# Feed-forward weights laid out in stationary order, a three-part normalisation on ScalarE, and a second product that runs two tiles behind

## What is computed

```
xn = layernorm(x)                                        # over 512, eps 1e-5
s  = attention(xn, wq, wk, wv, wo)                       # 32 query heads, 8 kv heads, head 128, RoPE, window 128
W1, W3 (1376 x 512), W2 (512 x 1376) = dequant_q40(w, s) # high and low nibble of a packed int, one scale per 64
g  = silu((silu(xn @ W1.T) * (xn @ W3.T)) @ W2.T)
out = x + s * g
```

## Time and profile before

| | us |
|---|---|
| median of 3 runs | 878.67 |
| lowest, highest | 878.37, 880.2 |
| the profiled execution, whole | 877.86 |
| its span in the trace | 876.1 |
| TensorE busy in the span | 840.6 (96%) |
| VectorE, ScalarE, GpSimd busy | 600.6, 469.7, 390.2 |
| granted TensorE clock, mean | 0.998 |

### The profile page before, as it was taken

One profiled execution on the slowest core, in us unless ns is written; L12 is line 12 of the kernel. 1 busy time (PEld: TensorE's weight loads), 2 busy tenths in 40 slices (PEclk: granted clock), 3 DMA queues, 4 the chain that ended last, 5 costly groups with the idle time before them and its releaser, 6 DMA issues.

```text
span 876.1 us, 13995 instructions
## 1 busy us (share of the span) xinstructions
PE 840.6 (96%) x4252; PEld 701.8 (80%) x4252; DVE 600.6 (69%) x1621; ACT 469.7 (54%) x1133; POOL 390.2 (45%) x303
## 2 busy tenths in 40 slices
PE   3999999999989999999999999999999999999887
PEld 3777888888767888888888888888888888888765
DVE  7953554433569677775968586677858676875895
ACT  2474121132577557574756666485748557574641
POOL 0144121124545436552644464184435436552892
PEclk9999999999999999999999999999999999999999
DMA  6200001002010201200120111012000201200211
GB/s 195 56 18 8 13 24 51 19 1 72 1 41 9 74 1 48 73 1 1 48 72 0 48 36 35 0 48 72 0 27 21 72 0 48 72 0 0 61 62 60
DMA packets 40224, 32.55 MB, mean 37 GB/s; under 512 B 5056, under 2 KB 32384, under 8 KB 40192
## 3 DMA queue, kind: packets, MB, share of 16 engines
q1 hardware_dynamic: 40192, 32.16, 12.5%
HBM read 30.05 MB, written 2.10 MB: 37 GB/s over the span
## 4 chain that ended last, share of the span: by engine, by line
PE 82%; DVE 8%; POOL 3%; issue 3%; ACT 3%; DMA 0%; SPq 0%; ACTq 0%; POOLq 0%; DVEq 0%
PE bank L966 25%; PE bank L968 24%; PE bank L967 24%; PE bank L1106 5%; PE bank L1086 3%; DVE probs L815 2%; POOL acc L338 1%; ACT W2raw L433 1%; POOL swap L321 1%; PE bank L986 1%; PE bank L1076 1%; DVE xl L655 1%; POOL acc L342 0%; POOL q L325 0%; DMA xn<-in_L_attn_x 0%
## 5 line engine op out<-in xcount | busy, mean ns | idle before, releaser
L321 POOL TENSOR_TENSOR swap<-swap,cst 128x512 f32<-128x512 f32 x80 | 103.9, 1298 | 248.8 <-ACT swap L488 247.9
L966 PE MATMUL bank<-xh,wih 128*128 128x512 f32 x384 | 158.5, 413 | 0.2 <-DVE q L783 0.2
L968 PE MATMUL bank<-xh,wil 128*128 128x512 f32 x384 | 151.0, 393 | 0.0
L967 PE MATMUL bank<-xl,wih 128*128 128x512 f32 x384 | 150.3, 391 | 0.0
L815 DVE TENSOR_SCALAR probs<-probs,rinv 128x128 f32<-128x128 f32 (+1 forms) x256 | 129.1, 546 | 4.6
L515 ACT ACTIVATE probs<-probs,nmx 128x128 f32<-128x128 f32 (+1 forms) x256 | 113.5, 445 | 33.8 <-DVE nmx L804 33.4
L523 ACT ACTIVATE ph<-bank 128x512 fp32r<-128x512 f32 x96 | 55.6, 597 | 112.2 <-PE bank L1106 110.9
L966 PE MATMUL bank<-woh,oh 128*128 128x512 f32 x256 | 100.4, 392 | 0.3 <-DVE ol L832 0.3
L968 PE MATMUL bank<-woh,ol 128*128 128x512 f32 x256 | 99.9, 390 | 0.0
L967 PE MATMUL bank<-wol,oh 128*128 128x512 f32 x256 | 99.9, 390 | 0.0
L287 POOL TENSOR_TENSOR hl<-act_h,hh 128x512 fp32r<-128x512 f32 x22 | 29.9, 1361 | 148.2 <-ACT hh L416 148.2
(11 more groups left out here) (102 smaller groups left out, 1828.0 us busy)
## 6 DMA issues: line engine op xcount, KB each, us to landing
raw<-in_L_attn_wq SPq DMA_DIRECT2D x32, 256.0 KB, 2.8
raw<-in_L_attn_wo SPq DMA_DIRECT2D x32, 256.0 KB, 2.9
packed<-in_L_ffn_w SPq DMA_DIRECT2D x20, 128.0 KB, 2.2
xn<-in_L_attn_x SPq DMA_DIRECT2D x8, 256.0 KB, 3.5
raw<-in_L_attn_wk SPq DMA_DIRECT2D x8, 256.0 KB, 3.0
raw<-in_L_attn_wv SPq DMA_DIRECT2D x8, 256.0 KB, 2.7
raw<-in_L_attn_x SPq DMA_DIRECT2D x8, 256.0 KB, 2.7
out<-gate SPq DMA_DIRECT2D x8, 256.0 KB, 2.0
```

What stands on the lines that cost most here:

```text
L321: nc.gpsimd.tensor_tensor(v, v, spread(sin.unsqueeze(1), P, 2, SEQ), ALU.mult).then_inc(sin_done, 1)
L966: nc.tensor.matmul(out_, sh, mh, start=(i == 0), stop=False)
L967: nc.tensor.matmul(out_, sh, ml, start=False, stop=False)
L968: m = nc.tensor.matmul(out_, sl, mh, start=False, stop=(i == n - 1))
```

## The change

The host hands the packed weights over in another order: W1 and W3 with the inner dimension on partitions (the packed row of 64 is loaded twice, once for the high and once for the low nibbles), W2 with the hidden dimension on partitions. No value is computed on the host; scales are repeated so that each weight has its own, and the scales of W1 and W3 are spread over 64 partitions by the load itself. Unpacking is a shift left by 24 or 28 (by partition or by column) and an arithmetic shift right by 28, then one multiplication. The result is what the matmuls need, so all transposes of weights go, and the high and low parts are made from SBUF instead of PSUM.

- Normalisation in three parts: tiles 0-1, 2-3 and 4-7; the normalising pass moves to ScalarE (scale and bias). The square-root table is loaded ahead by a dummy activation.
- TensorE begins with tile 0 in quarters of 256 tokens; tiles 0 and 1 run their first halves before their second halves.
- The hidden buffer has four slots; `w2_mult(u)` runs behind tile 2u+3, for every u, and uses four PSUM banks (banks 0 and 1, which the turned weights had, come free).
- W2 is unpacked tile by tile, tile t-2 during tile t; the last three during tile 10, and the loads of them wait for buffers (`load2`).
- The loops over feed-forward tiles are written out.

```
-            def w13_turn(t, s2_):          # 8 transposes for a tile: gone
-            def w2_turn(t):                # 4 transposes for a tile: gone
+            def load13(t, m):
+                wait(sp, W13_done, 2 * t + m - 3)
+                s = t % 2
+                for half in range(2):
+                    rows = slice(half * HALF, half * HALF + HALF)
+                    sp.dma_start(pk[rows, s, m, :], w13[:, t, m, :]).then_inc(w13_in[s][m], 16)
+                    sp.dma_start(sc[rows, s, m, :], s13[half, t, m:m + 1, :].to_broadcast([HALF, PK])) \
+                        .then_inc(w13_in[s][m], 16)
+            def load2(t):
+                wait(sp, W2_done, t - 1)
+                sp.dma_start(pk2[:, t % 2, :], w2[t]).then_inc(w2_in[t % 2], 16)
+                sp.dma_start(sc2[:, t % 2, :], s2[t]).then_inc(w2_in[t % 2], 16)
...
+            def norm(i):                   # ScalarE
+                act.wait_ge(ln_small, 6 * part_of(i) + 6)
+                nc.scalar.activation(xn[:, i, :], xn[:, i, :], ACT.Identity, bias=std[:, 0, i:i + 1],
+                                     scale=std[:, 3, i:i + 1]).then_inc(xn_done, 1)
...
+            for t in range(2, FT - 1):     # ScalarE
                 silu(t, 0)
+                hid_hi(t, 0)
+                w2_hi(t - 2)
                 silu(t, 1)
+                hid_hi(t, 1)
+                if t + 2 < FT:
+                    w13_hi(t + 2, 0)
+                    w13_hi(t + 2, 1)
             silu(10, 0)
+            hid_hi(10, 0)
+            w2_hi(FT - 3)
+            w2_hi(FT - 2)
+            w2_hi(FT - 1)
             silu(10, 1)
+            hid_hi(10, 1)
...
+            def dequant13(t, m):           # VectorE
+                nc.vector.tensor_scalar(nib[:, m, :], pk[:, s, m, :], shc[:, 4:5], shc[:, 5:6],
+                                        ALU.logical_shift_left, ALU.arith_shift_right).then_inc(nib_done, 1)
+                nc.vector.tensor_tensor(W13[:, m, :], nib[:, m, :], sc[:, s, m, :], ALU.mult).then_inc(W13_done, 1)
+            def w13_lo(t, m):
+                nc.vector.tensor_tensor(W13l[:, t % 2, m].rearrange("p t n -> p (t n)"), W13[:, m, :],
+                                        W13h[:, t % 2, m].rearrange("p t n -> p (t n)").bitcast(f32),
+                                        ALU.subtract).then_inc(W13l_done, 1)
+            def dequant2(t):
+                nc.vector.tensor_tensor(nib2[:, :].rearrange("p (e j) -> p e j", j=4),
+                                        pk2[:, s, :].rearrange("p (e j) -> p e j", j=4),
+                                        spread(shc[:, 0:4].unsqueeze(1), P, P, 4), ALU.logical_shift_left)
+                nc.vector.tensor_scalar(nib2[:, :], nib2[:, :], 28, None, ALU.arith_shift_right)
+                nc.vector.tensor_tensor(W2[:, s, :], nib2[:, :], sc2[:, s, :], ALU.mult).then_inc(W2_done, 1)
...
+            for t in range(2, FT):         # VectorE
+                if t + 2 < FT:
+                    dequant13(t + 2, 0)
+                    dequant13(t + 2, 1)
+                hid(t, 0)
+                dequant2(t - 2)
+                if t == FT - 1:
+                    dequant2(t - 1)
+                    dequant2(t)
+                hid(t, 1)
+                if t + 2 < FT:
+                    w13_lo(t + 2, 0)
+                    w13_lo(t + 2, 1)
+                if t > 2 and t % 2:
+                    ffn_add((t - 3) // 2)
...
+            for t in range(2, FT - 1):     # GpSimd
+                hid_lo(t, 0)
+                w2_lo(t - 2)
+                hid_lo(t, 1)
+            hid_lo(FT - 1, 0)
+            w2_lo(FT - 3)
+            w2_lo(FT - 2)
+            w2_lo(FT - 1)
+            hid_lo(FT - 1, 1)
...
+            def w2_mult(u, pair):          # TensorE
+                pe.wait_ge(W2l_done, 2 * u + len(pair))
...
+            x_turn(0)
+            x_turn(1)
+            w13_start(0, 0)
+            x_turn(2)
+            x_turn(3)
+            w13_start(0, 1)
+            w13_start(1, 0)
+            w13_start(1, 1)
+            w13_mult(1, 0, 0, {3: lambda: x_turn(4)})
+            x_turn(5)
+            w13_mult(1, 0, 1, {2: lambda: x_turn(6), 3: lambda: x_turn(7)})
+            for t in range(2):
+                w13_mult(t, 1, 0)
+                w13_mult(t, 1, 1)
+            w13_tile(2)
+            for u in range(FT // 2 - 1):
+                w13_tile(2 * u + 3)
+                w2_mult(u, (0, 1))
+                w13_tile(2 * u + 4)
+            w2_mult(FT // 2 - 1, (0, 1))
```

More of the change, by code:

```diff
@@ L221, in _ @@
[L221 to L230, removed]
+            load13(1, 1)
+            for t in range(2, FT):
+                for m in range(2):
+                    load13(t, m)
+                if t == 2:
+                    sp.dma_start(cst[:, 0:C_ID], const[:, 0:C_ID]).then_inc(const_in, 16)
+                load2(t - 2)
@@ L274, in _, with w13_first @@
         def _(pool):
[L276 to L288, removed]
+            def w13_first(t, m):
+                pool.wait_ge(W13h_done, 2 * t + m + 1)
+                nc.gpsimd.tensor_tensor(W13l[:, t, m].rearrange("p t n -> p (t n)"), W13[:, m, :],
+                                        W13h[:, t, m].rearrange("p t n -> p (t n)").bitcast(f32),
+                                        ALU.subtract).then_inc(W13l_first, 1)
@@ L290, in _ @@
+            for t in range(2):
+                for m in range(2):
+                    w13_first(t, m)
             hid_lo(0, 0)
+            hid_lo(1, 0)
+            hid_lo(0, 1)
             hid_lo(1, 1)
[L292 to L296, removed]
@@ L400, in w13_hi @@
[L400 to L405, removed]
-            def silu(t, half):
-                act.wait_ge(ab_ps, 4 * t + (2 * half + 1))
-                wait(act, hl_done, 2 * t + (half - 1))
-                nc.scalar.activation(act_h[:, half, :], bank[2 + 2 * half][:, :], ACT.Silu).then_inc(silu_done, 1)
@@ new lines, in _ @@
+            x_hi(0)
+            x_hi(1)
+            root(1)
+            norm(2)
+            norm(3)
+            w13_hi(0, 1)
+            x_hi(2)
+            x_hi(3)
+            w13_hi(1, 0)
+            root(2)
+            for i in range(4, NT):
+                norm(i)
+            w13_hi(1, 1)
+            for i in range(4, NT):
+                x_hi(i)
+            silu(0, 0)
+            hid_hi(0, 0)
+            silu(1, 0)
+            hid_hi(1, 0)
+            silu(0, 1)
+            hid_hi(0, 1)
@@ L994, in w13_mult, with w13_start, w13_tile @@
+            def w13_start(m, part):
+                cols = slice(2 * part * P, (2 * part + 2) * P)
+                pe.wait_ge(W13l_first, m + 1)
+                pe.wait_ge(xl_done, 2 * part + 2)
+                i = three(bank[2 + m][:, cols],
+                          [(W13h[:, 0, m, d, :], W13l[:, 0, m, d, :], xh[:, d, cols], xl[:, d, cols])
+                           for d in range(DT)])
+                if part:
+                    i.then_inc(ab_ps, 1)
+            def w13_tile(t):
                 for half in range(2):
-                    wait(pe, h_done, 2 * t + (half - 1))
@@ L1007, in w2_turn @@
[L1007 to L1016 removed]
+                        w13_mult(t, half, m)
```

494 lines of the change are left out of this document (213 added, 281 removed).

## The result

The changed kernel is slower: 886.25 us (median of 6 runs, 881.98 to 886.76) against 878.52 (6 runs, 877.99 to 880.2), ratio 1.007, 95% interval 1.0053 to 1.0087. The forecast was 869.9 with a range to 876. The profiled execution took 883.83 us, its span 881.8; the granted TensorE clock was 0.986 of full speed where it had been 0.998, and in the other five runs 0.983 to 0.990.

A forecast was written before the change was run, and what follows sets the result against it. TensorE, busy 96% of the span, was taken as the bound. Overhead removed 16.0, stalls 9.9, start 1.6 and end 1.1 gave 16.0 - 9.9 + 1.6 + 1.1 = 8.8 us less: 869.1 profiled, 869.9 median, range 861 to 876.

The forecast's parts named there:

- What the removed work is worth: Tile 2 to the attention: 153.4 us of matmuls stay out of 169.4; the other 16.0 are overhead the change removes.
- the stalls: TensorE's new waits for W2's low part, ahead of the five w2_mult: 9.9 us in sum.
- The upper bound of 16: Most the five W2 waits could total: each half as long again and loads 1 us late at every pair.
- The waits: TensorE waiting for W2's low part: 2.3 us for u = 0, 1.3 each for u = 1 to 3, 3.7 in tile 10.
- Rival B: Transfers decide: each pair 1.5 us later still, or the start loses its gain; 2.8 us less, 875.9; chance 0.13.
- Being held: VectorE operations with two SBUF inputs and GpSimd's exclude each other for a whole instruction; dequant2's product held until 9.7.
- The start: Up to tile 2: a chain through VectorE and ScalarE; tile 2 begins at 43.7 instead of 45.30, 1.6 us earlier.
- The two stalls behind it: TensorE's waits before tile 2: 1.6 us for W3's low part and 2.6 for act_h.
- The end: Last single tile of the second product: four banks end TensorE's waits for VectorE's adds, 1.1 us gained.
- C: Slower than before: VectorE becomes the bound of the feed-forward, 20 us lost against 18.7 gained; 880, chance 0.06.

The follow-up runs named there:

- the variant: Changed kernel with W2's unpacking put first in its tile on VectorE, ScalarE and GpSimd: 862.12 us, ratio 0.9816 to the kernel before; 861.12 when run again.
- the filled waits: Changed kernel with 48 extra 512-column matmuls ahead of TensorE's waits for W2's low part: 878.23 us, ratio 0.9994 to the kernel before.
- the loads edit: Changed kernel with W1/W3 loads ahead of the waiting W2 load in SyncE's list: 875.1 us, ratio 0.9957; on top of W2's unpacking first, 861.11 us.
- the half tile: Changed kernel with w2_mult(u), u = 0 to 3, half a tile later in TensorE's list: 872.19 us, ratio 0.9917 to the kernel before.
- put in: Three idle times on TensorE, made by GpSimd fills, added to the kernel with W2's unpacking first: 881.61 us, ratio 1.0025 to the kernel before.
- the start edit: Kernel with W2's unpacking first, plus silu table and W3's high part of tile 1 earlier: 859.15 us, again 860.45; with W1/W3 loads earlier too, 860.02.

## Why the prediction was wrong

Against the profiled execution: forecast 869.1, measured 883.8, 14.7 too little. The median is 16.4 above its forecast: it lies 2.4 above the profiled execution, where I had put it 0.8 above. For these 1.6 us there is no trace.

- **What the removed work is worth: right.** Forecast 153.4 us of matmuls between tile 2 and the attention; without a wait, in the variant, the stretch takes 152.8 (45.54 to 198.39). 16.0 were to be had there.
- **The failed step: the stalls were priced as idle time only.** "Stalls: 3.9 + 2.3 + 3.7 = 9.9." should have been idle time and what it does to the clock. That is 8.1 us, more than half of the error, and the filled waits show them by themselves. Behind the start the kernel before has no slow matmul, and its longest wait there is 1.1 us. But the start had the sign, and I read past it: 16 turns behind the wait of 9.6 us take 3.65, and 16 behind the wait of 2.2 take 2.02. Start to start that is 0.21 us and 0.11, half speed and full. I asked for waits of 1.3 to 3.7 us and left the clock out of the forecast and of the bounds. The upper bound of 16 is also summed too low by its own conditions: half as long again is 14.9, and 1 us more at each of five pairs makes 19.9. The page "TensorE: Matmul & The Clock Gate" of the Trainium skill, section "HAM oscillation — how this bites in real kernels", has the mechanism (a stall sends the engine back to the slow clock, and the next stretch of matmuls starts slow), and I had not weighed it. The runs here agree with it.
- **The waits: right in place and mechanism, too small by 4.** Forecast 2.3, 1.3, 1.3, 1.3, 3.7; measured 4.9, 2.7, 2.7, 0.2, 3.3 (13.9 of idle time, 14.7 in distances between starts). Two terms are off. Rival B's loads were on the path for u = 0 to 2, and with them sent earlier these waits are 2.2, 1.1 and 1.5, close to the forecast: I had given the second W1/W3 load 1 us of margin, with 0.45 us for an issue that takes 0.6, eight in a row. And u = 3 has no `dequant13` ahead of it, as t + 2 is past the last tile; I gave it the same 1.3 as its neighbours. Tile 10 was right.
- **Being held: right.** The product takes 1.67 to 1.69 in nine of eleven, where I had counted it as held.
- **The start: 1.7 us too good.** Tile 2 at 45.4, forecast 43.7. VectorE waited 0.8 for the first scales to land, and a pass of the normalisation took 0.80 on ScalarE, 0.71 start to start, where I took about 0.6. The two stalls behind it were forecast at 1.6 and 2.6, and came at 1.9 and 2.6.
- **The end: right.** 1.2 us, forecast 1.1: the last single tile takes 5.45 us in place of 6.62, and the attention's list lost nothing.
- **The rivals.** B's mechanism was there and C's sign, but for another reason than the one C named: VectorE is not short of time between tile 2 and the attention (reordering alone frees TensorE there completely). A chance of 0.07 for slower was too sure: the forecast stalls all had the same unpriced follow-up, so they failed together.

## What to carry to other kernels

When a change takes work off the bounding engine and adds waits to it, price a wait of TensorE as its idle time plus the slow matmuls behind it (here 1.5 to 2.8 us for each wait of 2.7 to 4.9), and look for the order in which nothing is needed the moment it is made: 24 us came back here by moving one unpacking up in the lists of three engines. Follow a queue's order as you follow an engine's: a load behind another one's wait inherits that wait. An operation that moves from PSUM to SBUF operands gains a competitor in GpSimd.

## What the runs showed of the hardware

- Between tile 2 and the attention TensorE's clock fell to half at every wait of 2.7 us or longer (2.7, 2.7, 3.3, 4.9 in the changed kernel, 3.3 with the loads edit, 3.9 with the half tile, 4.3 and 5.3 put in), behind none of 1.5 or shorter, and in between sometimes: behind 2.2 in one run, not behind 2.5 and 2.56 in two others. Behind the two waits of 2.7 it fell only after TensorE had begun again: the first slow start comes 1.4 and 1.6 us behind the restart, which is easy to miss. The wait for act_h at 34 us, 2.6 in all profiles but those with the start edit, is followed by six to eight slow starts in four of the profiles and by none in the others, the changed kernel's among them. What decides it I did not find. It costs 1.6 us. With the 2 us near the end it may be a part of why the changed kernel's runs spread from 881.98 to 886.76, where the clock was 0.983 to 0.990; only one of these runs has a trace.
- TensorE begins at half speed too, and for a time that differs from run to run. In the changed kernel's profile the 256-column matmuls of the first quarters start 0.21 us apart up to 14 us, and 0.12 apart from 17.8 on. In the variant's second profile they are 0.21 apart up to 23.6. The windows give a granted clock of 1.00 for such a stretch, so at the start of a trace the distance between starts is what to read.
- GpSimd holds a single-source int shift of VectorE too. In the changed kernel one of `dequant2` takes 1.49 in place of 0.43, beside `w2_lo` (VectorE's row, then GpSimd's):

```profile
203.44 1.49 DVE L721 TENSOR_SCALAR nib<-nib 128x512 int32<-128x512 int32 x1
```

```profile
203.35 1.30 POOL L300 TENSOR_TENSOR W2l<-W,W2h 128x512 fp32r<-128x512 f32 x1 [1.29 <-ACT W2h L445]
```

It ends 0.28 after GpSimd does. That agrees with the second half of what the page "SBUF — State Buffer" of the Trainium skill has in its section "Who interferes with whom", which no row had shown; whether the shift runs in a two-port mode, no run shows.
- SyncE needs 0.6 us to issue one of the loads of 128 KB to 64 partitions (the queue's rows above); I had taken 0.45 from the loads of the kernel before.
